# Four of nine experts take the output product in high and low halves, two pairs on ScalarE and GpSimd; the other five stay float32

## The reference, cut to what matters

```python
scores = softmax(xf @ gate_w.T)                       # 8 experts
topk_w, topk_i = top_k(scores, 2)
topk_w = topk_w / (topk_w.sum(-1, keepdims=True) + 1e-20)
combine = zeros((T, E)).at[arange(T)[:, None], topk_i].add(topk_w)
h1 = relu(einsum('th,ehf->tef', xf, w1) + b1)
eo = einsum('tef,efh->teh', h1, w2) + b2
y  = einsum('te,teh->th', combine, eo)
shared = relu(xf @ sw1 + sb1) @ sw2 + sb2             # a ninth, for every token
return y + shared
```

## Time and profile before

| | |
|---|---|
| median of 3 runs | 676.63 us (674.88 to 676.95) |
| profiled run | 676.65 us, of which the span from first to last instruction is 674.9 us |
| busy: PE / DVE / ACT / POOL | 639.7 / 475.4 / 393.2 / 289.6 us |
| TensorE clock granted, mean | 0.991 of full |
| chain that ended last, PE's share | 86% |

### The profile page before, as it was taken

How to read it: one execution, slowest core, us unless ns; L and a number is a source line. 1 busy time by engine, 2 the same in 40 slices (tenths; PEclk the granted TensorE clock), 3 DMA queues, 4 the chain that set the end, 5 groups by cost and what they waited for, 6 DMA issues and landing times.

```text
span 674.9 us, 15767 instructions
## 1 busy us (share of the span) xinstructions
PE 639.7 (95%) x5684; PEld 557.6 (83%) x5684; DVE 475.4 (70%) x1432; ACT 393.2 (58%) x1350; POOL 289.6 (43%) x486
## 2 busy tenths in 40 slices
PE   8887799999999999999999999999999999998986
PEld 7777598898979798897979888897979889786764
DVE  4645867777686777777687777778687777775532
ACT  3476575656657475656658565665747565665210
POOL 2464435445445354355444544444535535534200
PEclk9999899999999999999999999999999999999999
DMA  6000020302003020302103030200402030201220
GB/s 219 25 2 24 2 93 21 102 25 101 25 13 114 1 103 24 103 25 65 62 2 118 9 103 24 103 25 2 125 1 104 24 103 2 87 17 34 70 84 29
DMA packets 16748, 37.34 MB, mean 55 GB/s; under 512 B 1504, under 2 KB 13728, under 8 KB 14624
## 3 DMA queue, kind: packets, MB, share of 16 engines
q1 hardware_dynamic: 16672, 36.35, 16.6%
HBM read 33.14 MB, written 3.20 MB: 54 GB/s over the span
## 4 chain that ended last, share of the span: by engine, by line
PE 86%; DVE 6%; ACT 3%; POOL 2%; issue 1%; DMA 1%; ACTq 0%; POOLq 0%; DVEq 0%
PE ps_mix L637 13%; PE ps_fill L756 13%; PE ps_fill L413 12%; PE ps_fill L414 10%; PE ps_fill L415 10%; PE ps_dots L626 9%; PE ps_av L645 7%; PE ps_fill L566 6%; DVE x2T_lo L1133 1%; PE ps_fill L737 1%; ACT x2T_hi L870 1%; DMA spread<-weights 1%; PE ps_fill L738 1%; DVE aT L1076 1%; PE ps_fill L743 1%
## 5 line engine op out<-in xcount | busy, mean ns | idle before, releaser
L787 ACT ACTIVATE ex<-ps_dots,negmax 128x92 f32<-128x92 f32 x384 | 124.1, 341 | 4.1 <-DVE negmax L1057 3.7
L1205 POOL TENSOR_TENSOR sum<-sq 92x384 f32<-92x384 f32 x64 | 64.3, 1005 | 128.4 <-ACT sq L795 128.4
L637 PE MATMUL ps_mix<-mixk,probs 128*92 128x128 f32 x768 | 98.8, 280 | 3.0 <-DVE aT L1078 2.7
L1199 POOL TENSOR_TENSOR probs<-ex,rinv 128x552 f32<-128x552 f32 x64 | 70.8, 1107 | 52.3 <-DVE rinv L1063 52.3
L637 PEld LDWEIGHTS ps_mix<-mixk,probs 128*92 128x92 f32 x768 | 88.1, 163 | 6.2 <-issue 2.5
L756 PE MATMUL ps_fill<-act,w_sb 128*128 128x368 f32 x288 | 91.6, 472 | 0.0
L1152 DVE SCALAR_TENSOR_TENSOR act<-ps_fill,b_neg,spread 128x368 f32<-128x368 f32 x128 | 70.5, 591 | 24.2 <-PE ps_fill L415 17.2
L787 ACT ACTIVATION_READ_ACCUMULATOR ex<-ps_dots,negmax 128x1 f32 x384 | 81.4, 212 | 0.0
L756 PEld LDWEIGHTS ps_fill<-act,w_sb 128*128 128x128 f32 x288 | 54.3, 190 | 31.1
L626 PE MATMUL ps_dots<-xT,yT 128*64 128x92 f32 x1536 | 73.6, 245 | 2.9 <-ACT ex L787 2.9
L626 PEld LDWEIGHTS ps_dots<-xT,yT 128*64 128x64 f32 x1536 | 64.1, 137 | 6.1 <-ACT ex L787 3.6
(11 more groups left out here) (174 smaller groups left out, 1457.0 us busy)
## 6 DMA issues: line engine op xcount, KB each, us to landing
spread<-weights SPq DMA_DIRECT2D x16, 1472.0 KB, 6.2
xin<-in_x SPq DMA_DIRECT2D x16, 320.0 KB
out<-ostage SPq DMA_DIRECT2D x16, 128.0 KB, 3.0
out<-ostage SPq DMA_DIRECT2D x16, 56.0 KB, 3.7
xin<-in_x SPq DMA_DIRECT2D x16, 52.0 KB
act<-w_raw SPq DMA_DIRECT2D x1, 576.0 KB, 7.2
w_sb<-w_raw SPq DMA_DIRECT2D x1, 576.0 KB, 8.5
qkv<-qk_raw SPq DMA_DIRECT2D x1, 512.0 KB, 5.3
```

The source lines that it names most:

```text
L637: last = pe.matmul(ps_mix[0:N, c // HALF, o:o + 128], probs[:, (s - 1) % 2, c, :], mixk[:, :, :].rearrange("p g i -> p (g i)"), start=True ...
L787: last = act.activation(ex[:, s % 2, c, :], ps_dots[:, c // HALF, o:o + N], ACT.Exp, bias=negmax[:, c:c + 1], accum_out=sums[:, s % 2, c:c ...
L1199: pool.tensor_tensor(probs[:, s % 2, :, :], ex[:, s % 2, :, :], rinv[:, s % 2, :].unsqueeze(2).broadcast_to([128, CHUNKS, N]), ALU.mult).t ...
L1205: pool.tensor_tensor(sum4[:, :, :, :], sq[:, :, 0:4, :], sq[:, :, 4:8, :], ALU.add)\
```

## The change

`UNITS` becomes `("H0", "H1")`. H0 stands for experts 0 and 1, H1 for experts 2 and 3. For each, ACT writes the rounded copy of both experts' `act1` into `act1_split` (one instruction, 736 columns), and POOL then writes the difference (one instruction, 736 columns). In `YF`, five experts (4 to 8) keep the float32 matmul and come first, and the four halved ones follow with three float32r products each. `prepE` splits four matrices of `w2` too. `RT` waits for that in the iterations that are written out. H0 and H1 get places in `STEPS` and in the three `ORDERS_END`.

```diff
+    ("mix", 1), ("exb", 1), ("av", 1), ("inv", 1), ("dots", 2), ("sq", 1), ("ev", 1), ("max", 2), "H0", "Z7", "OP",
+    ("rstd", 1), ("scale", 1), "shift", "H1", "TK", "TH2", "Z4", ("exa", 2), "TH", ("mix", 2), ("av", 2), "NH2",
...
-UNITS = ()
+UNITS = ("H0", "H1")
...
-    ("av", 1), ("ev", 1), "Z7", "OP", "Z2", "TH2", "Z3", "NH2", "TX2", "RT", "R2", "R3", "YF", "CT", "OT", "hold",
+    ("av", 1), ("ev", 1), "Z7", "OP", "Z2", "TH2", "Z3", "NH2", "TX2", "RT", "R2", "R3", "H1", "YF", "CT", "OT",
+    "hold",
...
-    "Z8", "Z3", "Z2", "Z0", "Z1", "Z5", "Z4", "Z6", "Z7", "YF", "OT",
+    "Z8", "Z3", "Z2", "Z0", "Z1", "Z5", "H1", "Z4", "Z6", "H0", "Z7", "YF", "OT",
...
+        w2_split = split("w2_split", [128, 2 * len(UNITS), 128])
...
-                    if direct(G):
-                        experts = [other for other in order(G) if other in EXPERTS + (f"Z{E}",)]
-                        for other in experts:
-                            wait_emptied(pe, other, G)
-                            e = int(other[1])
-                            last = pe.matmul(ps[:, 0:W], w2_sb[:, e, :], act1[:, e, :], start=False,
-                                             stop=other == experts[-1])
...
+                    halved_experts = EXPERTS[0:2 * len(UNITS)]
+                    for other in [other for other in order(G) if other in EXPERTS + (f"Z{E}",)]:
+                        e = int(other[1])
+                        if other not in halved_experts:
                             wait_emptied(pe, other, G)
+                            pe.matmul(ps[:, 0:W], w2_sb[:, e, :], act1[:, e, :], start=False, stop=False)
+                    units = [unit for unit in order(G) if unit in UNITS]
+                    for ahead, unit in enumerate(units):
+                        pe.wait_ge(units_ready, len(UNITS) * g + ahead + 1)
+                        for e in (2 * int(unit[1]), 2 * int(unit[1]) + 1):
+                            last = products(ps[:, 0:W], [w[:, e, :] for w in w2_split],
+                                            [m[:, e, :] for m in act1_split], False,
+                                            unit == units[-1] and e % 2 == 1)
...
-                    for n, ((hi, lo), raw) in enumerate([(w1_split, w1_sb)]):
+                    for n, ((hi, lo), raw) in enumerate([(w1_split, w1_sb), (w2_split, w2_sb[:, 0:2 * len(UNITS), :])]):
```

More of the change, by code:

```diff
@@ L77 @@
     "Z6", ("inv", 0), "XE", ("dots", 1), ("rstd", 0), ("max", 1), ("scale", 0), "Z8", "Z0", "Z1", ("exa", 1), "XO",
[2 rows of a table removed]
-    ("exb", 2), ("dots", 3), "TX2", ("sq", 2), ("max", 3), "V2", ("exa", 3), ("inv", 2), "RT", "R2", ("rstd", 2),
-    "V3", "R3", ("scale", 2), "YF", "TX", "CT", ("ev", 2), ("mix", 3), "XS", "Y6", "Y5", "Y3", ("sq", 3), "Y2",
-    "hold", ("exb", 3), "Y1", ("inv", 3), "OT", ("av", 3), ("ev", 3), "Y4", ("rstd", 3), "Y7", ("scale", 3), "Y0",
-    "V0", "BS",
[6 rows of a table added]
 ]
@@ L108 @@
 LAST = NG + 2
-DIRECT = FIRST
 KEEP_BUSY = {(FIRST, "XE"): 13, (FIRST, "TK"): 10, (FIRST, "TX"): 13, (LAST - 2, ("mix", 0)): 8, (LAST - 2, "TH2"): 4,
@@ L140 @@
     ("inv", 0), ("ev", 0), ("dots", 1), ("rstd", 0), ("scale", 0), "Z6", "Z1", ("av", 1), ("max", 1), ("mix", 1),
-    ("ev", 1), ("exa", 1), ("sq", 1), ("exb", 1), "Z7", ("inv", 1), "OP", ("dots", 2), ("max", 2), ("rstd", 1), "Z8",
-    ("scale", 1), ("exa", 2), "TH2", "Z3", ("exb", 2), "NH2", ("av", 2), ("mix", 2), ("dots", 3), ("max", 3),
-    ("ev", 2), ("sq", 2), "TX2", ("inv", 2), ("exa", 3), "RT", "V3", ("exb", 3), "R2", ("rstd", 2), "R3",
+    ("ev", 1), ("exa", 1), ("sq", 1), ("exb", 1), "Z7", ("inv", 1), "H0", "OP", ("dots", 2), ("max", 2), ("rstd", 1),
[2 rows of a table added]
     ("scale", 2), "YF", "shift", "CT", ("mix", 3), ("sq", 3), "V2", "OT", ("inv", 3), ("rstd", 3), ("av", 3), "hold",
@@ L146 @@
 ], [
-    "Z8", ("mix", 0), ("sq", 0), ("av", 0), ("ev", 0), "Z5", "Z1", "Z0", ("rstd", 0), ("scale", 0), "Z4", "Z6",
-    ("av", 1), ("ev", 1), "Z7", "OP", "Z2", "TH2", "Z3", "NH2", "TX2", "RT", "R2", "R3", "YF", "CT", "OT", "hold",
+    "Z8", ("mix", 0), ("sq", 0), ("av", 0), ("ev", 0), "Z5", "Z1", "Z0", ("rstd", 0), ("scale", 0), "H0", "Z4", "Z6",
+    ("av", 1), ("ev", 1), "Z7", "OP", "Z2", "TH2", "Z3", "NH2", "TX2", "RT", "R2", "R3", "H1", "YF", "CT", "OT",
+    "hold",
 ], [
-    "Z8", "Z3", "Z2", "Z0", "Z1", "Z5", "Z4", "Z6", "Z7", "YF", "OT",
+    "Z8", "Z3", "Z2", "Z0", "Z1", "Z5", "H1", "Z4", "Z6", "H0", "Z7", "YF", "OT",
 ]]
@@ L485, in low_units @@
             eng.tensor_tensor(lo, act1[:, two, :], hi.bitcast(F32), ALU.subtract).then_inc(units_ready, 1)
-        def direct(G):
-            return G >= DIRECT if isinstance(G, int) else DIRECT <= STEADY
         def bank(step):
@@ L683, in do @@
                 if step == "RT" and isinstance(G, int):
-                    pe.wait_ge(experts_ready, 2)
+                    pe.wait_ge(experts_ready, 3)
                 operands = {
@@ L750, in do @@
                     pe.matmul(ps[:, 0:W], b2_all[:, :], combT[:, :], start=True, stop=False)
-                    if direct(G):
-                        experts = [other for other in order(G) if other in EXPERTS + (f"Z{E}",)]
-                        for other in experts:
+                    halved_experts = EXPERTS[0:2 * len(UNITS)]
+                    for other in [other for other in order(G) if other in EXPERTS + (f"Z{E}",)]:
+                        e = int(other[1])
+                        if other not in halved_experts:
                             wait_emptied(pe, other, G)
-                            e = int(other[1])
-                            last = pe.matmul(ps[:, 0:W], w2_sb[:, e, :], act1[:, e, :], start=False,
-                                             stop=other == experts[-1])
-                    else:
-                        units = [unit for unit in order(G) if unit in UNITS]
-                        for ahead, unit in enumerate(units):
-                            pe.wait_ge(units_ready, len(UNITS) * g + ahead + 1)
-                            k = int(unit[1])
-                            for e in range(2 * k, min(2 * k + 2, E + 1)):
-                                last = products(ps[:, 0:W], [w[:, e, :] for w in w2_split],
-                                                [m[:, e, :] for m in act1_split], False,
-                                                unit == units[-1] and e == min(2 * k + 1, E))
+                            pe.matmul(ps[:, 0:W], w2_sb[:, e, :], act1[:, e, :], start=False, stop=False)
[6 more added lines that the diff above has]
+                                            unit == units[-1] and e % 2 == 1)
                     last.then_inc(done, 1)
```

## The result

The changed kernel took 674.45 us (median of 22 runs, 671.40 to 676.57), the kernel before 676.92 (22 runs, 674.66 to 680.33): ratio 0.9958, 95% interval 0.9946 to 0.9971. The change is worth 2.5 to 2.8 us (by the medians and by the ratio), where 6.4 were forecast. The profiled run took 675.11 us with a span of 673.0.

A forecast was written before the change was run, and what follows sets the result against it. PE, busy 639.7 of 674.9 us, was taken to bound the kernel. Saving 7.1 us, less 0.2 and 0.5 lost, gave 676.65 - 6.4 = 670.3 us; own range 669 to 671.5, with rivals 668.8 to 674.5.

The forecast's parts named there:

- What bounds the kernel; what PE saves: Steady iteration: the chain runs over PE; each expert switched in YF saves 0.118 us, four save 0.47 us.
- What ACT and POOL pay: H0 and H1: an ACT copy takes 0.80 us and a POOL subtraction 1.75 us, both hidden from PE in steady iterations.
- The start: prepE: POOL's longer w2 split makes DVE's L954, perhaps two small neighbours, wait; 0.5 us lost (0.25 to 0.8).
- G = 16: POOL's H1 subtraction blocks DVE's routing, so combine ends at about 650.6, not 649.02; iteration gives +0.2 instead of -0.47 us.
- 15 iterations x 0.47 = 7.1 us: Sum: full YF saving in the 13 steady iterations (G = 2 to 14) and in G = 15 and G = 17.
- Rival (b), the clock: Added PE waiting at the start or in G = 16 lengthens or adds half clock: 1.5 to 3 us more; chance 0.08.
- Rival (a): Y steps behind YF, on banks DVE and ACT empty, give back half the saving: about 673.5 us; chance 0.12.
- (c): POOL's subtractions take 2.5 us each and come late for the layer norm: slower, about 681 us; chance 0.05.
- (d): YF's halves cost as much as float32 because each product's weight load shows through: 677.3 us; chance 0.02.

The follow-up runs named there:

- e5: The changed kernel with YF all float32 as before; H0, H1 and the w2 split are made but unused: 679.52 us, ratio 1.0030.
- e6: The kernel before plus only POOL's split of four experts' w2 in prepE, used by nobody: 678.49 us, ratio 1.0017.
- e2: The changed kernel with H1 of G = 16 moved behind NH2, ahead of the routing: 674.15 us, ratio 0.9958.
- e4: The kernel before with PE's side alone: twelve float32r products of existing operands replace four float32 matmuls in YF, nothing halved: 670.43 us, ratio 0.9906.
- e8: The changed kernel with w2 split late, H1 of G = 16 early, and fillers of the last two iterations 512 columns wide and fewer: 673.29 us, ratio 0.9948.
- e12: The changed kernel with w2 split late, H1 of G = 16 early, and filler products of iteration LAST - 2 cut in two: 671.64 us, ratio 0.9922.
- e14: The same kernel as e12, run again as control beside e13: 671.12 us, ratio 0.9909.
- e1: The changed kernel with w2 split at the end of iteration 0 instead of in prepE: 673.39 us, ratio 0.9941.
- e7: The changed kernel with the 33 filler products of iteration LAST - 2 each cut in two: 673.11 us, ratio 0.9941.
- e11: The changed kernel unaltered, run again for a second profile: 673.31 us, ratio 0.9956.
- e13: e12's kernel plus seven filler products on PE in G = 15 while it waits for x2T: 670.53 us, ratio 0.9898.
- e9: The kernel before with the 33 filler products of iteration LAST - 2 each cut in three: 680.93 us, ratio 1.0064.

## Why the prediction was wrong, step by step

- **What bounds the kernel; what PE saves.** Right in the mechanism. YF lost 0.46 us (forecast 0.47), the steady iteration 0.42 to 0.43. The remaining 0.04 us went in steps of some hundredths over PE's products of the iteration; no single wait shows.
- **What ACT and POOL pay.** Right: 0.81 and 1.76 us against 0.80 and 1.75, no wait of PE for the halves or for NH2, and e5's period (38.43 us beside 38.41) bears it out.
- **The start.** The mechanism was right (mixc in place of the L954 named, its neighbour), and the step lost 0.51 us against 0.5. What arrives at x2T_lo of G = 1 is 0.8 us between profiles with the same half clock, and e6 put the split alone at 1.2 us (interval 0.1 to 2.2). The half clock there differs by 3.4 us and more from profile to profile; that the split adds to it is not shown.
- **G = 16.** Right in mechanism and size: combine 1.5 us late, this stage +0.3 us against +0.2. But PE's new wait there was taken for the whole price. In three of four profiles the clock falls behind it, within the next 4 us.
- **The step that failed: "15 iterations x 0.47 = 7.1 us".** The steady ones are worth 0.43, 0.5 us less over the twelve, and G = 15 and G = 17 were taken "by the same reading" of one steady iteration. The account says what came in place of the term. The stage with the YF of G = 14 and 15 gave 0.1 us and not 0.9: in one of the two profiles of after (8 of 9 with the halves used) a fall of the clock takes 1.7 us back. The transfer ahead of the last stage cost 0.8 (1.6 us in one of the two) where nothing was put. The stage with the YF of G = 17 lost 0.2 and not gained 0.5: it takes 10.8 us where the clock stays whole from G = 16 on (e2 to e4, e8, e12 to e14) and 11.1 to 11.6 where it falls (after, e1, e7, e11). With the 0.4 us outside of the span these make 3.2 of the 3.7 us that are missing. The two ends were costed for their own operations only, not for what PE's waits do there.
- **Rival (b), the clock**, was the nearest: it named G = 16 and the start and priced 1.5 to 3 us. It had 0.08, on the ground that both waits were short beside others. The ground doesn't hold: behind a gap of 1.34 us, which the kernel before has too, the fall cost 1.68 us in e14 beside e13. Half the length of all stretches at half clock within the span comes to 4.7 to 8.5 us in the five profiles with a float32 YF, to 7.0 to 11.1 in the nine with the halves used, and to 3.1 in e13, in which the start happened to have none before 76 us.
- **Rival (a)** named the right result (673.5 us) with a cause that isn't there: the steady iteration keeps 0.43 of the 0.47, so the Y steps behind YF don't give half back. (c) and (d) are out, by the rows of POOL and of YF.
- **Not in the sum at all:** the 0.3 us outside of the span, and the 46th piece of PE's program.

The measured 674.45 us lies outside of the forecast's own range (669 to 671.5) and inside 668.8 to 674.5 by 0.05 us. The latter is luck: the range was stretched that far for rivals (a) and (b), and the saving is less than half of the 6.4 us forecast. The chance of 0.89 for faster was right in sign: the whole interval of the ratio lies below 1, though with 0.42% it is near what can be told from no change.

## What to carry to other kernels

Cost the unrolled iterations at both ends by their own rows: a saving read from the steady iteration need not hold there, since one fall of the clock to half behind a wait of PE takes back as much as four such savings (1.7 us here). Where PE must wait near its end, try filling the gap with products into a free bank, and compare the granted clock in several profiles of both kernels. Keep POOL's long SBUF instructions off the stretches in which DVE works through small ones. When PE's program grows, look at where its last code pieces land among the transfers that something waits for.

## What the runs showed of the hardware that I had not expected

- The same idle gap of PE (1.34 us ahead of the gate products of G = 15) left the clock at 1.00 in all five profiles with a float32 YF and was followed by 0.50 in eight of nine with the changed one. With seven fillers in it the clock stayed at 1.00, in one profile.
- A fetch of 16 KB of program code (q8) near the end of two transfers brought the smaller of them in 7.0 to 7.2 us instead of 5.4 to 6.1, six times out of six, and the larger in 8.0 instead of 6.5, three times out of six. With the same fetch 0.8 and 1.3 us after the issue the larger took 6.57 and 6.74 us.
- DVE's tensor_scalar on 128x8, with two SBUF operands, stood for POOL's subtraction as the tensor_tensor step of G = 16 did (1.71 us against 0.18): 0.74 us against 0.23 when POOL was quiet.
- Filler products of 122 columns started 0.109 us apart, those of 368 columns 0.167 (the first fillers of G = 16, in e9 and in before): a third of the columns for two thirds of the time, so narrow fillers cost PE time.
- The time outside of the span was 2.1 us in every kernel with two more instructions an iteration on ACT and on POOL and 1.8 in every one without (medians of their runs). The reason was not looked for.
